# Two attentions with 8-wide heads: unnormalised probabilities with their sums from a column of ones, queries and keys two batches ahead and split on POOL, and another order

## The reference, cut to what matters

```python
x = L0_attn_x                                  # (16, 256, 128)
xn = _layernorm(x)
x = x + _L0_attn_ref(xn, ...) + _L0_ffn_ref(xn, ...)      # causal, scale 1/8; int8 matmul
xn = _layernorm(x)
x = x + _L1_attn_ref(xn, ...) + _L1_ffn_ref(xn, ...)      # not causal, scale 1/sqrt(8)
...                                                       # layers 2 and 3
# both attentions, b=16, n=256, 16 heads of 8
q = _rope(heads(x @ Wq)); k = _rope(heads(x @ Wk)); v = heads(x @ Wv)
scores = einsum('bhqd,bhkd->bhqk', q, k) * SCALE (+ mask)
attn = softmax(scores, axis=-1)
out = einsum('bhqk,bhkd->bhqd', attn, v)
return out.reshape(b, n, 128) @ Wo + bo
```

## Time and profile before

| | us |
|---|---|
| median of 3 runs | 3639.64 |
| lowest, highest | 3634.89, 3640.42 |
| the profiled execution | 3634.8 |
| its span, first to last instruction | 3633.5 |
| of it: layer 0 attention, from the first `scores` to the last `add` | 382.5 |
| of it: layer 1 attention, the same | 383 |

### The profile page before, as it was taken

One profiled execution on the slowest core, in us unless ns is written; L12 is line 12 of the kernel. 1 busy time (PEld: TensorE's weight loads), 2 busy tenths in 40 slices (PEclk: granted clock), 3 DMA queues, 4 the chain that ended last, 5 costly groups with the idle time before them and its releaser, 6 DMA issues.

```text
span 3633.5 us, 74423 instructions
## 1 busy us (share of the span) xinstructions
PE 3228.4 (89%) x24511; PEld 2336.4 (64%) x24511; DVE 2613.4 (72%) x5857; ACT 2503.4 (69%) x8041; POOL 2286.8 (63%) x2118
## 2 busy tenths in 40 slices
PE   5999868887764999699999799999999999999997
PEld 4666645555553888566756576767676767767775
DVE  7888868887377556644434677887777788777786
ACT  5888848886322555553533588888888888888885
POOL 4777747775122666330200788888888888888884
PEclk9999969998876999899999899999999999999999
DMA  3221132221000000300000000000000000000000
GB/s 94 71 65 65 50 104 66 67 65 33 1 1 0 1 1 1 100 13 1 1 1 1 12 2 2 2 2 2 2 2 2 2 2 2 2 2 1 2 2 24
DMA packets 54907, 78.41 MB, mean 22 GB/s; under 512 B 5952, under 2 KB 43648, under 8 KB 54272
## 3 DMA queue, kind: packets, MB, share of 16 engines
q1 hardware_dynamic: 54528, 73.65, 6.4%
HBM read 54.76 MB, written 18.87 MB: 20 GB/s over the span
## 4 chain that ended last, share of the span: by engine, by line
PE 43%; POOL 5%; ACT 5%; DVE 3%; issue 3%; DVEq 0%; ACTq 0%; POOLq 0%
PE psum L1928 8%; PE psum L1943 7%; PE psum L1918 7%; PE psum L1966 4%; POOL attn_p L2285 3%; PE psum L1415 3%; ACT attn_p L2040 3%; PE psum L1875 2%; POOL attn_qf L2279 2%; PE psum L1340 2%; PE psum L1426 2%; PE psum L1487 1%; PE psum L1506 1%; PE psum L1320 1%; DVE attn_nm L2160 1%
## 5 line engine op out<-in xcount | busy, mean ns | idle before, releaser
L2040 ACT ACTIVATE attn_p<-psum,attn_nm 128x256 f32<-128x256 f32 x1536 | 709.5, 478 | 250.8 <-DVE attn_nm L2160 246.6
L2285 POOL TENSOR_TENSOR attn_p<-attn_p,attn_rinv 128x512 f32<-128x512 f32 x768 | 783.4, 1041 | 133.2 <-DVE attn_rinv L2167 133.2
L612 POOL TENSOR_TENSOR sb_a_p<-sb_a_p,sb_a_rinv 128x512 f32<-128x512 f32 x512 | 529.9, 1045 | 196.9 <-DVE sb_a_rinv L500 194.5
L569 ACT ACTIVATE sb_a_p<-psum,sb_a_nm 128x256 f32<-128x256 f32 x1024 | 480.3, 507 | 74.5 <-DVE sb_a_nm L493 73.0
L2160 DVE TENSOR_REDUCE attn_nm<-psum 128x2 f32<-128x512 f32 x768 | 491.4, 681 | 20.0 <-PE psum L1918 19.7
L1943 PE MATMUL psum<-attn_pt,attn_v 128*64 128x256 f32 x3072 | 416.3, 391 | 32.7 <-DVE attn_ql L2179 28.7
L1928 PE MATMUL psum<-sb_kept,attn_p 128*128 128x128 f32 x3072 | 426.7, 280 | 7.9 <-POOL attn_p L2285 7.8
L1928 PEld LDWEIGHTS psum<-sb_kept,attn_p 128*128 128x128 f32 x3072 | 328.3, 140 | 163.2 <-issue 93.1
L408 PE MATMUL psum<-sb_kept,sb_a_p 128*128 128x128 f32 x2048 | 308.8, 286 | 75.5 <-DVE sb_a_pt L506 57.8
L493 DVE TENSOR_REDUCE sb_a_nm<-psum 128x2 f32<-128x512 f32 x512 | 343.7, 675 | 15.8 <-PE psum L392 10.9
L2040 ACT ACTIVATION_READ_ACCUMULATOR attn_p<-psum,attn_nm 128x1 f32 x1536 | 320.2, 208 | 0.0
(11 more groups left out here) (400 smaller groups left out, 7999.7 us busy)
## 6 DMA issues: line engine op xcount, KB each, us to landing
sb_a_spread<-a_spilled SPq DMA_DIRECT2D x128, 256.0 KB, 3.1
a_spilled<-sb_a_part_hi SPq DMA_DIRECT2D x64, 128.0 KB
a_spilled<-sb_a_part_lo SPq DMA_DIRECT2D x64, 128.0 KB
sb_x<-in_L_attn_x SPq DMA_DIRECT2D x4, 512.0 KB, 6.2
sb_wg<-in_L_ffn_Wg SPq DMA_DIRECT2D x1, 2048.0 KB, 10.3
sb_wu<-in_L_ffn_Wu SPq DMA_DIRECT2D x1, 2048.0 KB, 15.1
...
```

What stands on the lines that cost most here:

```text
L569: ins = act.activation(Pr[:, p % 3, e, t, :], S(p, e)[:, t * N:(t + 1) * N], ACT.Exp, bias=nm[:, p % 4, e, t:t + 1], accum_out=rsum[:, p % ...
L612: pool.tensor_tensor(P3, P3, spread(rinv[:, p % 4, e, :], N), ALU.mult).then_inc(normed.sem, 1)
L2040: ins = act.activation(Pr[p % 3][:, e, t, :], S(p, e)[:, t * N:(t + 1) * N], ACT.Exp, bias=nm[:, p % 4, e, t:t + 1], accum_out=rsum[:, p % ...
L2285: pool.tensor_tensor(P3, P3, spread(rinv[:, p % 4, e, :], N), ALU.mult).then_inc(normed.sem, 1)
```

## The change

- **No normalising.** `invert` and `norm` are gone, and `exps` has no `accum_out`. The transposes (`turn`) wait for `exped`. v's unused columns are set so that column 8 of each head's 32 is 1.0 (`v_filled`); row 8 of the head's 32 rows in O is then the sum of its probabilities.
- **O is one group of four heads.** Each `weigh` starts anew in O. Then `copy_sums` (ACT) copies O to SBUF, `turn_back` (PE, two transposes) turns it into OT, the other half of the same bank, and `settle` (DVE, a reciprocal of 128x8 and a product of 128x64) divides and writes to `o`. The next `weigh` waits for `settled`. After a batch `turn_out` (PE, two transposes) turns `o` in bank M, `copy_out` copies it, and `through_wo` uses Wo as it is; the permuted copies of Wo and their two matmuls and copies in `prepare8` go.
- **Queries and keys.** `project` and `rope_turn` for batch b+2 stand in steps 0 and 2 of batch b. POOL's `part` now does the sum and the split, and POOL's `lay` does what ACT's did. In the preparing steps POOL lays q and k of batch 0 ahead of its adds of steps 4 and 5. The high and low parts and the DRAM boxes are doubled.
- **Order.** `weigh` moves from odd to even steps, `turn_back` stands in odd steps, `settle` at the head of DVE's even steps, `add` at the head of step 7.

The diff, cut to its core:

```diff
@@ attention8, PE @@
         def project(b, j):
...
-            elif b >= 3:
-                pe.wait_ge(*added(b - 3))
+            elif b >= 4:
+                pe.wait_ge(*added(b - 4))
+            elif b == 2:
+                pe.wait_ge(*turned_q(3))
...
+        def turn_out(b):
...
+            pe.wait_ge(*settled((b + 1) * PB // 2 - 1))
+            for t in range(TB):
+                mm = pe.transpose(M[:, t * P:(t + 1) * P], o[b % 2][:, t, :], c.ident)
+            mm.then_inc(out_turned.sem, 1)
...
         def turn(p, e):
-            pe.wait_ge(*normed(2 * p + e))
+            pe.wait_ge(*exped(2 * p + e))
...
-                if b:
-                    pe.wait_ge(*out_moved(b - 1))
+            if i:
+                pe.wait_ge(*settled(i - 1))
...
+        def turn_back(i):
+            pe.wait_ge(*summed(i))
+            for t in range(TB):
+                mm = pe.transpose(OT[:, t * P:(t + 1) * P], sums[i % 2][:, t * P:(t + 1) * P], c.ident)
+            mm.then_inc(backed.sem, 1)
@@ attention8, DVE @@
-        def hi_lo(b, j):
...
-        def invert(p, e):
...
+        def settle(i):
+
+            b, j = divmod(i, PB // 2)
+            dve.wait_ge(*backed(i))
...
+            src = OT.rearrange("p (t r c) -> p t r c", t=TB, c=ROW)
+            c.dve_own(dve.reciprocal(rinv[:, :, :], src[:, :, :, HD8]))
+            out = o[b % 2][:, :, j * ROW:(j + 1) * ROW].rearrange("p t (r d) -> p t r d", d=HD8)
+            dve.tensor_tensor(out, src[:, :, :, 0:HD8], rinv[:, :, :].unsqueeze(3).to_broadcast((P, TB, 4, HD8)),
+                              ALU.mult).then_inc(settled.sem, 1)
@@ attention8, ACT @@
             for t in range(TB):
                 ins = act.activation(Pr[:, p % 3, e, t, :], S(p, e)[:, t * N:(t + 1) * N], ACT.Exp,
-                                     bias=nm[:, p % 4, e, t:t + 1], accum_out=rsum[:, p % 4, e, t:t + 1])
+                                     bias=nm[:, p % 4, e, t:t + 1])
...
+        def copy_sums(i):
+            act.wait_ge(*weighed(i))
...
+            act.copy(sums[i % 2][:, :], O).then_inc(summed.sem, 1)
@@ attention8, POOL @@
+        def part(b, j):
...
             pool.tensor_tensor(rot[:, :], t1[:, :], t2[:, :], ALU.add).then_inc(rotated.sem, 1)
+            pool.wait_ge(*rotated(2 * b + j))
+            c.pool_own(pool.tensor_copy(hi, rot[:, :]))
+            pool.tensor_tensor(lo, rot[:, :], hi.bitcast(F32), ALU.subtract).then_inc(parted.sem, 1)
+
+        def lay(b, j):
+            pool.wait_ge(*landed[j](32 * (b + 1) - 1))
...
+            pool.tensor_copy((q, ks)[j][b % 2][:, :, :], spreads[j][:, :, :]).then_inc(laid.sem, 1)
 
         for j in range(steps):
...
+            if j in (4, 5):
+                lay(0, j - 4)
             if beside:
                 beside.pool_step(j)
```

More of the change, by code:

```diff
@@ L270, in __init__, with prepare8 @@
         self.tmp, self.br1 = sb("a8_tmp", [P, 2, D]), sb("a8_br1", [P, 2])
-        self.wo = [sb(f"a8_wo{i}", [P, D]) for i in range(2)]
-def prepare8(c, t, w0, w1, bias1, perm):
+def prepare8(c, t, w0, w1, bias1):
     nc = c.nc
     pe, act, pool = nc.tensor, nc.scalar, nc.gpsimd
-    made, kept, zeroed = c.steps("w_made", 2), c.steps("w_kept", 2), c.steps("v_zeroed", 2)
+    made, kept, filled = c.steps("w_made", 2), c.steps("w_kept", 2), c.steps("v_filled", 2)
     pair = lambda bank, at: bank[:, at:at + 2 * D].rearrange("p (k d) -> p k d", d=D)
@@ L338, in attention8 @@
     v_ready = c.steps("v_parted", TB * B)
-    scored, weighed = c.steps("scored", NP), c.steps("weighed", NP // 2)
-    maxed, exped, inverted, normed, turned = (c.steps(k, 2 * NP) for k in ("maxed", "exped", "inverted", "normed", "turned"))
+    scored = c.steps("scored", NP)
+    weighed, summed, backed, settled = (c.steps(k, NP // 2) for k in ("weighed", "summed", "backed", "settled"))
+    maxed, exped, turned = (c.steps(k, 2 * NP) for k in ("maxed", "exped", "turned"))
     even, odd = c.steps("even_moved", NP), c.steps("odd_moved", NP)
-    out_moved, through, added = c.steps("out_moved", B), c.steps("through_wo", B), c.steps("added", B)
+    out_turned, out_moved, through, added = (c.steps(k, B) for k in ("out_turned", "out_moved", "through_wo", "added"))
     def pe_program():
@@ L442, in pe_program @@
                 turn(p - 2, 0)
+            if 2 <= p < NP + 2:
                 turn(p - 2, 1)
+            if p % 2 == 0 and 4 <= p < NP + 4:
+                weigh((p - 4) // 2)
             if p % 2 and 5 <= p < NP + 5:
-                weigh((p - 5) // 2)
-            if j == 0 and b + 1 < B:
-                project(b + 1, 1)
+                turn_back((p - 5) // 2)
+            if j in (0, 2) and b + 2 < B:
+                project(b + 2, j // 2)
             elif j == 4 and b + 1 < B:
@@ L450, in pe_program @@
             elif j == 5 and b:
+                turn_out(b - 1)
+            elif j == 6 and b:
                 through_wo(b - 1)
-            elif j == 6 and b + 2 < B:
-                project(b + 2, 0)
     def dve_program():
@@ L522, in dve_program @@
                 lay_v(0, 1)
-            elif j == 3:
-                rope_turn(1, 0)
+            elif j in (3, 4):
+                rope_turn(1, j - 3)
             if beside:
                 beside.dve_step(j)
-        for p in range(NP + 7):
+        for p in range(NP + 8):
             b, j = divmod(p, PB)
+            if p % 2 == 0 and 6 <= p < NP + 6:
+                settle((p - 6) // 2)
+            if j == 7 and b:
+                add(b - 1)
             if p < NP:
                 maxima(p, 0)
-            if 1 <= p < NP + 1:
-                invert(p - 1, 1)
             if p < NP:
@@ L587, in act_program @@
                 beside.act_step(j)
-        for j in range(2):
-            lay(0, j)
-        for p in range(NP + 5):
+        for p in range(NP + 7):
             b, j = divmod(p, PB)
-            if b and j == 4:
+            if p % 2 and 5 <= p < NP + 5:
+                copy_sums((p - 5) // 2)
+            if j == 6 and b:
                 copy_out(b - 1)
@@ L657, in attention8 @@
     sp_program()
-    c.meet(added, laid, normed, weighed, out_moved)
+    c.meet(added, laid, weighed, out_moved)
     if beside:
```

172 lines of the change are left out of this document (69 added, 103 removed).

## The result

| | before | changed |
|---|---|---|
| median, us | 3637.53 (3634.89 to 3640.42) | 3572.35 (3568.38 to 3573.42) |
| ratio, 95% interval | | 0.9819 [0.9802, 0.9836] |
| the profiled execution's span | 3633.5 | 3567.1 |

The changed kernel is 65 us faster (1.8%). The forecast was 3590 us, the range 3556 to 3626.

What follows compares the result with a forecast made beforehand. No engine was full; a ring of waits through ACT, DVE, POOL and PE held the attentions. Layer 0 -12, layer 1 -42, start +3, ends +1: -50 us from the median 3639.6, forecast 3590, range 3556 to 3626.

Steps and rivals of the forecast that it cites:

- the ring of sums, reciprocals and products: Both 8-wide attentions: ACT, DVE, POOL and PE wait for each other; PE stands still 2.75 and 5.15 us a batch.
- PE's added transposes: Four `turn_back` and one `turn_out` a batch at 0.32 us each: 1.6 us more PE work, ends 0.6 and 3.2.
- Rival 2: Added transposes cost 0.64 us each, 1.6 us a batch more, +51 us: 3641, no change; chance 0.08.
- Layer 0: First 8-wide attention: batch falls from 23.45 to 22.7 us, PE's need plus 0.4 of waits; -12 us.
- Layer 1: Second 8-wide attention: batch falls from 23.45 to 20.6 us, 0.7 of it waits, first batch given nothing; -42 us.
- The split: Layer 1: cast and difference hold DVE 1.44 us twice a batch; PE's 1.55 us stall behind it taken to be gone.
- `settle` and the chain in one bank: DVE's `settle` takes 0.4 us, four a batch; each link from weights to next weights has 0.8 us to spare.
- POOL's copy: POOL's two copies of 1024 columns a batch take 1.1 to 2.9 us each, hidden a whole batch early.
- The ends: Start of layer 0 +2 us (-1 to +5), start of layer 1 +1, after each layer's last scores +0.7.
- 1, the clock: Layer 1: PE still idles once a batch, losing half of 3.4 us to low clock: 25 us, 3615; chance 0.15.
- 3: `turn_back` waits for ACT's copy, 0.9 us in each of 128 places: +65 us, 3705, slower; chance 0.10.
- 4, more than forecast: PE without a wait, `turn_back` at 0.2: batches of 21.7 and 19.3 us, 3550 to 3560; chance 0.10.

Runs made afterwards that it cites:

- b_no_norm: Kernel before with the normalising taken out of both 8-wide attentions (no sums, reciprocals, POOL products or division): 3570.55 us, ratio 0.9796.
- b_split_pool: Kernel before with only the high/low split of queries and keys moved from DVE to POOL: 3624.61 us, ratio 0.9947.
- a_split_dve: Changed kernel with the split put back on DVE, one step behind the rope product: 3605.59 us, ratio 0.9898.
- a_split_dve_apart: Changed kernel with the split back on DVE and POOL's copies made to wait for step 5's scores of the batch before: 3587.33 us, ratio 0.9854.
- a_lay_late: Changed kernel with POOL laying batch 0's queries and keys behind its adds of steps 6 and 8 in layer 0's preparing steps: 3569.95 us, ratio 0.9801.
- a_one_ahead: Changed kernel with queries and keys projected one batch ahead in place of two, at the same steps: 3666.03 us, ratio 1.0062.

## Why the prediction was right, and where it was off

The measured 3572 us lie in the range, 18 us under the forecast. Both layers moved the way that was forecast, for want of waits for POOL and DVE; 11 us of the miss are in layer 0 and 7 in layer 1.

**What bounds the kernel.** The forecast took the gain from the ring of sums, reciprocals and products. b_no_norm shows that the normalising was the bound, and b_split_pool that PE still waits for POOL's products when DVE is free of the split. How the gain divides between the waits of the ring and the products' collisions with DVE, of which the prediction knew nothing, stays open.

**PE's added transposes.** 0.32 taken, ends 0.13 and 0.64: 0.31 us ahead of scores, 0.21 for one of the two that stand side by side once a batch. Rival 2 needed 0.64.

**Layer 0**, forecast -12, measured -22.9. Two terms were mis-sized. PE's need was put at 22.3 and 0.4 us of waits added; the need is 22.45 (a projection is 1.06, `project_v` 0.64) and the waits are none. Against the steady 23.66 of before that is (23.66 - 22.47) x 15.9 = 19. And I compared a need, which is a steady batch, with 23.45, a mean over the layer that holds its shorter ends. Mean against mean it is (23.45 - 22.01) x 15.9 = 22.9; in the changed kernel the first batch takes 19.2 us (21.1 in its second profile) and the fifteenth, which has nothing left to project, 20.4, against 21.5 and 23.8 before.

**Layer 1**, forecast -42, measured -48.8. The batch was forecast at 20.6 with 0.7 us of waits and is 20.85 with 0.8. It was set against the mean of 23.45 where the steady batch before is 23.69, and by luck the two errors cancel: 2.85 us a batch forecast, 2.84 measured. Of the 6.8 us missed half is the term that failed, the first batch, given nothing because of the low clock: it took 22.1 us before and takes 18.6 now. The clock rises at 492.3, 9 us behind the first scores (483.31), where before it rose at 517.9, 15.8 us behind them (502.05). In these stretches PE was busy for 8.97 of 8.97 us in the changed kernel and for 14.58 of 15.84 before; more about why it rises sooner no run here tells. Most of the rest lies in the fifteenth batch, which has no projections: 18.1 us where it was 23.9, 3.0 more than a steady batch gains.

**The split.** I held its 1.44 us to be DVE's work; 0.70 is. The rest was the collision with POOL's products, which stops when these go. The step's result came out for a reason other than the one I gave: b_split_pool shows that the split's move alone brings layer 1 nothing, a_split_dve that with the products gone it is worth 1.3 to 1.5 us a batch, and a_split_dve_apart that half of this is again a collision, with POOL's copies.

**`settle` and the chain in one bank.** 0.4 taken. DVE's timeline of the changed kernel:

```profile
606.81 0.20 DVE L507 RECIPROCAL sb_a_rinv<-psum 128x8 f32<-128x8 f32 x1
607.04 0.22 DVE L509 TENSOR_TENSOR sb_a_o<-psum,sb_a_rinv 128x64 f32<-128x64 f32 x1
607.18 1.28 DVE L497 TENSOR_REDUCE sb_a_nm<-psum 128x2 f32<-128x512 f32 x2
```

607.18 - 606.81 = 0.37 us, and the weights behind it start at 607.60, without a wait. That the chain has little to spare shows when 0.70 us are put ahead of it.

**POOL's copy**, 1.1 to 2.9 taken: 1.04 us for 1024 columns, ACT's own pace, not four times a sum.

**The ends.** Start of layer 0 +2 forecast, +2.2 in this profile and +1.4 in the second; a_lay_late takes back 1.5 us of DVE's wait for POOL there, so POOL's early copy is at least most of it. Start of layer 1 +1 forecast, +0.1. Tails +0.7 each: +1.8 and +0.9 (+1.3 and +1.6 in the second profile), since the last group runs alone through eight links (weights, sums, turn back, division, turn out, copy, Wo, add). The changed kernel at the end of layer 0, from the last weights:

```profile
427.92 1.07 PE L429 MATMUL psum<-sb_a_pt,sb_a_v 128*32 128x256 f32 x16 [0.94 <-DVE sb_a_o L509]
429.06 0.37 ACT L573 COPY sb_a_sums<-psum 128x256 f32<-128x256 f32 x1 [2.11 <-PE psum L429]
...
429.49 0.44 PE L436 MATMUL psum<-sb_kept,sb_a_sums 128*128 128x128 f32 x2 [0.49 <-ACT sb_a_sums L573]
429.96 0.21 DVE L507 RECIPROCAL sb_a_rinv<-psum 128x8 f32<-128x8 f32 x1 [2.09 <-PE psum L436]
```

**The rivals.** 1, the clock: the stretches at 0.50 did not come back while PE was busy for 295.75 of 300 us; in a_one_ahead they came back with PE's waits for keys. 3: the wait is real and is kept away by one step's distance. 4, more than forecast, named PE without a wait and was right in that for layer 0; its batch of 21.7 us, with `turn_back` at 0.2, was too short.
